# A layer-norm, attention and LoRA layer on eight cores: the adapter selection moved behind the first matmul stage, other buffer counts, and one batched add per tile

## The reference

```python
q = einsum('bse,edh->bsdh', xn, Wq) + bq          # 32 heads of 128
k = einsum('bse,edh->bsdh', xn, Wk) + bk          # 8 heads, each repeated 4 times
v = einsum('bse,edh->bsdh', xn, Wv) + bv          # 8 heads, each repeated 4 times
scores = einsum('bsdh,bseh->bsde', q, k) / sqrt(128)
out = einsum('bsde,bseh->bsdh', softmax(scores), v)
y = einsum('bsd,od->bso', xn, weight) + bias      # 4096 -> 4096
lo = (xn A[adapter]^T) B[adapter]^T               # LoRA, rank 16, one of 3 adapters, by batch
```

## Time and profile before

| what | us |
|---|---|
| median of 3 runs | 1700.04 (1696.85 to 1707.28) |
| the profiled execution | 1697.85 |
| its span on the slowest core (core 4) | 1696.2 |
| spans of the 8 cores | 1690.7 to 1696.2 |
| DVE's first layer-norm reduction | 58.40 |
| stage 2's first matmul | 193.17 |
| stage 2's last matmul, xa's first | 859.59 |
| stage 4's first matmul | 908.28 |
| stage 5's first score matmul | 1381.70 |
| last store issued | 1680.5 |

### The profile page before, as it was taken

One profiled execution on the slowest core, in us unless ns is written; L12 is line 12 of the kernel. 1 busy time (PEld: TensorE's weight loads), 2 busy tenths in 40 slices (PEclk: granted clock), 3 DMA queues, 4 the chain that ended last, 5 costly groups with the idle time before them and its releaser, 6 DMA issues.

```text
span 1696.2 us, 20151 instructions; the slowest of 8 cores (1690.7 to 1696.2 us)
## 1 busy us (share of the span) xinstructions
PE 1380.9 (81%) x8600; PEld 690.2 (41%) x8705; DVE 270.0 (16%) x291; ACT 499.3 (29%) x497; POOL 185.4 (11%) x111
## 2 busy tenths in 40 slices
PE   0022699999999999999977999999999967756553
PEld 0011344444444444444433444444444435644442
DVE  2799200000000000000000000000000015544434
ACT  0255300111011103333343333333333345544442
POOL 1000011111111111111100111111110111011110
PEclk9999999999999999999987999999999975555555
DMA  5633087888888887777774777777777866899998
GB/s 113 84 120 148 1 75 75 75 78 75 78 79 79 79 78 76 75 75 75 75 89 74 71 72 72 72 74 75 75 75 75 84 81 91 105 113 133 120 132 117
DMA packets 503959, 144.77 MB, mean 85 GB/s; under 512 B 498672, under 2 KB 498704, under 8 KB 502800
## 3 DMA queue, kind: packets, MB, share of 16 engines
q0 software_dynamic: 337856, 101.53, 59.5%
q1 hardware_dynamic: 166016, 41.95, 15.1%
HBM read 207.20 MB, written 20.97 MB: 135 GB/s over the span
## 4 chain that ended last, share of the span: by engine, by line
PE 70%; DMA 11%; DVE 8%; issue 5%; ACT 3%; POOL 1%; SPq 0%; ACTq 0%; DVEq 0%; POOLq 0%
PE qk_ps L412 37%; PE f_ps L558 26%; PE s_ps L705 3%; DMA out<-xasm 3%; DVE lnst L272 2%; DVE lnst L267 2%; DVE sqscr L268 2%; ACT ebf L744 2%; DMA wsl<-wall 2%; PE a_ps L722 2%; DMA xasm<-x_in 1%; DMA qkscr<-tsb 1%; DMA a_all<-ah 1%; DMA out<-xasm_e 1%; PE f_ps L563 1%
## 5 line engine op out<-in xcount | busy, mean ns | idle before, releaser
L412 PE MATMUL qk_ps<-xnT,wsl 128*128 128x512 bf16 x3010 | 662.2, 380 | 5.6 <-ACT xnT L316 1.3
L412 PEld LDWEIGHTS qk_ps<-xnT,wsl 128*128 128x128 bf16 x3072 | 300.7, 98 | 366.9 <-issue 7.1
L558 PE MATMUL f_ps<-xnT,wsl 128*128 128x512 bf16 x2005 | 446.1, 380 | 4.6 <-ACT tsb L509 2.2
L558 PEld LDWEIGHTS f_ps<-xnT,wsl 128*128 128x128 bf16 x2048 | 198.1, 98 | 250.3 <-issue 16.9
L588 ACT ACTIVATE ffno<-f_ps,fb_sb 128x512 f16<-128x512 f32 x64 | 152.4, 2629 | 299.1 <-PE f_ps L563 299.1
L757 DVE RECIPROCAL rdb<-b_ps 128x16 f32<-128x16 f32 x64 | 16.2, 253 | 1345.7 <-PE b_ps L725 1273.7
L744 ACT ACTIVATE ebf<-s_ps 128x512 bf16<-128x512 f32 x256 | 139.7, 595 | 148.2 <-PE s_ps L705 147.9
L705 PE MATMUL s_ps<-qst,kst 8*128 8x128 bf16 x1024 | 136.1, 298 | 54.9 <-ACT ebf L744 38.7
L385 POOL DMA_DIRECT2D wsl<-wall x48 | 80.5, 1677 | 703.0 <-PE qk_ps L412 703.0
L442 ACT ACTIVATE qsks<-qk_ps,bqss 128x512 bf16<-128x512 f32 x16 | 36.8, 2537 | 354.0 <-PE qk_ps L412 354.0
L332 PE MATMUL tr_ps<-id_sb,xn 128*128 128x128 bf16 x256 | 33.9, 302 | 121.2 <-ACT xn L308 112.3
(11 more groups left out here) (65 smaller groups left out, 404.5 us busy)
## 6 DMA issues: line engine op xcount, KB each, us to landing
wsl<-wall POOLq DMA_DIRECT2D x80, 1024.0 KB, 12.2
xt<-x_in SPq DMA_DIRECT2D x8, 2048.0 KB, 8.8
xasm<-x_in POOLq DMA_DIRECT2D x10, 1024.0 KB, 14.1
out<-xasm SPq DMA_DIRECT2D x10, 1024.0 KB, 18.2
xasm_e<-x_in POOLq DMA_DIRECT2D x6, 1024.0 KB, 13.7
out<-xasm_e SPq DMA_DIRECT2D x6, 1024.0 KB, 16.4
qkscr<-tsb SPq DMA_DIRECT2D x16, 256.0 KB, 2.6
qst<-qkscr SPq DMA_DIRECT2D x32, 64.0 KB
```

What stands on the lines that cost most here:

```text
L412: mm = t.matmul(qk_ps[bank + half][:], wsl[ft % 2][:, c * P:(c + 1) * P], xnT[:, c * TPC + half * 512: c * TPC + (half + 1) * 512], start= ...
L558: t.matmul(f_ps[bank + half][:], wsl[ft % 2][:, c * P:(c + 1) * P], xnT[:, c * TPC + half * 512: c * TPC + (half + 1) * 512], start=(c == ...
```

## The change

Four things are changed together.

1. The adapter selection leaves the start. DVE begins with two short memsets (epsc, lnst) and the layer norm. The masks, bias sums and the memset of vall stand behind the last layer-norm tile. The broadcast of the masks (ps_h), the copy to hbc and the six mixing steps stand at the end of stage 2, between weight tile 47 and the xa matmuls. POOL loads a_all and the three B matrices, each now with a buffer of its own, behind weight tile 47; so its first two weight loads stand directly behind the seven small loads. TensorE waits for the small loads ahead of its first transpose.
2. Stage 1 has three x buffers instead of two.
3. Stage 5 has two buffers each for qst and kst instead of three; a chunk's load waits for the scores of the chunk two before.
4. In stage 5 the eight results of a tile go to slices of one buffer tmpa_full, and one add of 128x4096 after the eighth replaces the eight adds of 128x512. The wait for the x tile's load stands ahead of that add, and no longer ahead of the first step.

```diff
-        xt = [... for i in range(2)]
+        xt = [... for i in range(3)]
...
+        @block.gpsimd
+        def _(g):
...
+            g.dma_start(out=bsel_sb[:], in_=bsel_d).then_inc(GQ.h, 16)
+            GQ.n += 7 * 16
...
+        @block.vector
+        def _(v):
+            v.memset(epsc[:], EPS).then_inc(VEC.h, 1); VEC.n += 1
+            v.memset(lnst[:], 0.0).then_inc(VEC.h, 1); VEC.n += 1
...
             def _(sy):
                 for tt in range(NT):
-                    if tt >= 2:
-                        sy.wait_ge(SCA.h, p1_norm_mark[tt - 2])
+                    if tt >= 3:
+                        sy.wait_ge(SCA.h, p1_norm_mark[tt - 3])
...
             @block.tensor
             def _(t):
+                t.wait_ge(GQ.h, p0_gq)
                 for tt in range(NT):
...
+        @block.gpsimd
+        def _(g):
+            for ft in range(NQKV):
...
+            g.wait_ge(SCA.h, p1_trev_mark[NT - 1])
+            g.dma_start(out=a_all[:].rearrange("p (c a r) -> p c a r", c=CH, a=3),
+                        in_=ah_d.rearrange("c p a r -> p c a r")).then_inc(GQ.h, 16)
+            GQ.n += 16
+            for a in range(3):
+                g.dma_start(out=bsl[a][:], in_=bh_d[a]).then_inc(BS.h, 16)
+            BS.n += 3 * 16
...
                         mm.then_inc(TEN.h, 1)
                         TEN.n += 1
+                    t.wait_ge(VEC.h, p0b_mask_mark)
+                    t.matmul(ps_h[:], ones_r[:], h3b[:], start=True, stop=True)\
+                        .then_inc(TEN.h, 1)
+                    TEN.n += 1
                     t.wait_ge(VEC.h, p0_vec)
                     for c in range(CH):
...
                         if j == 0:
-                            s.wait_ge(VEC.h, p0_vec)
+                            s.wait_ge(VEC.h, p0b_mask_mark)
...
+                    s.wait_ge(TEN.h, p0_ten)
+                    s.activation(hbc[:], ps_h[:], AF.Copy).then_inc(SCA.h, 1)
                     s.wait_ge(TEN.h, p2_ten_end)
...
+                @block.vector
+                def _(v):
+                    v.wait_ge(SCA.h, p0_sca)
+                    v.wait_ge(GQ.h, p0b_gq)
...
-            qst = [p5sb(f"qst{i}", [NJ, 32 * P]) for i in range(3)]
-            kst = [p5sb(f"kst{i}", [NJ, 32 * P]) for i in range(3)]
+            qst = [p5sb(f"qst{i}", [NJ, 32 * P]) for i in range(2)]
+            kst = [p5sb(f"kst{i}", [NJ, 32 * P]) for i in range(2)]
...
                 for cki in range(4 * NT):
-                    if cki >= 3:
-                        sy.wait_ge(TEN.h, ten_schunk(cki - 3))
+                    if cki >= 2:
+                        sy.wait_ge(TEN.h, ten_schunk(cki - 2))
...
                 for tt in range(NT):
-                    v.wait_ge(XS[tt % 3].h, xs_mark(tt))
                     for sub in range(8):
...
-                        v.wait_ge(VEC.h, VEC.n)
-                        v.tensor_tensor(xasm[tt % 3][:, sub * 512:(sub + 1) * 512],
-                                        xasm[tt % 3][:, sub * 512:(sub + 1) * 512],
-                                        tmpa[0][:], ALU.add).then_inc(VEC.h, 1)
-                        VEC.n += 1
+                    v.wait_ge(XS[tt % 3].h, xs_mark(tt))
+                    v.wait_ge(VEC.h, VEC.n)
+                    v.tensor_tensor(xasm[tt % 3][:], xasm[tt % 3][:],
+                                    tmpa_full[:], ALU.add).then_inc(VEC.h, 1)
+                    VEC.n += 1
```

More of the change, by code:

```diff
@@ L83, in build @@
         vall = sbr("vall", [P, TPC * 9], BF16)
+        ps_h = ctx.enter_context(nc.psum_tensor("ps_h", [P, 3], F32))
         xasm_e = sbr("xasm_e", [P, P * 32], F32)
[L85 to L88, removed]
         xaT_guard = nc.sbuf_tensor("xaT", [16, TPC], BF16)
@@ L345, in build @@
         p1ctx.close()
+        aselt_guard = nc.sbuf_tensor("aselt", [P, CH * 16], BF16)
+        aselt = aselt_guard.__enter__()
+        bselt_guard = nc.sbuf_tensor("bselt", [16, 32 * P], BF16)
+        bselt = bselt_guard.__enter__()
+        p0bctx = ExitStack()
+        a_all = p0bctx.enter_context(nc.sbuf_tensor("a_all", [P, CH * 48], BF16, side="right"))
+        bsl = [p0bctx.enter_context(nc.sbuf_tensor(f"bsl{i}", [16, 32 * P], BF16, side="right"))
+               for i in range(3)]
+        p0b_vec0 = 2 + NT * 9
@@ L466, in build, with _ @@
                 p2_sca_end = SCA.n
-                assert p2_sca_end == p2_sca0 + 50
+                p0_sca = p2_sca0 + 49
+                assert p2_sca_end == p2_sca0 + 51
+                @block.vector
+                def _(v):
+                    v.wait_ge(SCA.h, p0_sca)
+                    v.wait_ge(GQ.h, p0b_gq)
+                    av = a_all[:].rearrange("p (c a r) -> p c a r", c=CH, a=3)
+                    sv = aselt[:].rearrange("p (c r) -> p c r", c=CH)
+                    v.tensor_scalar(sv, av[:, :, 0, :], hbc[:, 0:1], None, ALU.mult)\
+                        .then_inc(VEC.h, 1); VEC.n += 1
+                    for a in (1, 2):
+                        v.wait_ge(VEC.h, VEC.n)
+                        v.scalar_tensor_tensor(sv, av[:, :, a, :], hbc[:, a:a + 1], sv,
+                                               ALU.mult, ALU.add).then_inc(VEC.h, 1); VEC.n += 1
+                    for a in range(3):
+                        v.wait_ge(BS.h, 48)
+                        if a == 0:
+                            v.tensor_scalar(bselt[:], bsl[a][:], hbc[0:16, 0:1], None, ALU.mult)\
+                                .then_inc(VEC.h, 1); VEC.n += 1
+                        else:
+                            v.wait_ge(VEC.h, VEC.n)
+                            v.scalar_tensor_tensor(bselt[:], bsl[a][:], hbc[0:16, a:a + 1],
+                                                   bselt[:], ALU.mult, ALU.add)\
+                                .then_inc(VEC.h, 1); VEC.n += 1
+                        assert p0_b_vec_mark[a] == VEC.n, (a, p0_b_vec_mark[a], VEC.n)
+                assert VEC.n == p0_vec, (VEC.n, p0_vec)
             p3_ten0, p3_sca0 = TEN.n, SCA.n
```

253 lines of the change are left out of this document (108 added, 145 removed).

## The result

The changed kernel takes 1691.0 us (median of 12 runs, 1688.1 at the least) against 1701.98 for the kernel before: ratio 0.9942, interval 0.9928 to 0.9956. By the ratio it is faster by 10 us, and the interval doesn't reach 1; 22 were forecast, and over 1% (17 us) was held likely. Some runs of both kernels, and of three kernels further down, were disturbed and lie far above the rest; the medians take all runs in, the ratios leave these out.

A forecast was written before the change was run, and what follows sets the result against it. TensorE's weight streaming in stages 2 and 4 is 63% of the chain, untouched; time lies at the joints. -46.3 + 19.9 + 4 = -22.4 from 1697.85 gives 1675.5, put at 1677; range 1656 to 1694.

The forecast's parts named there:

- Part 1, the start: Stage 1 start: first layer-norm reduction moves from 58.40 to 12.1 us, 46.3 us gained.
- The lower bound: Start: weight tiles and third x tile hold x tile 0 back until 19.9, so the gain is 38.5 us.
- Part 2, the end of stage 2: Before the xa matmuls: TensorE idles 17.9 us through the selection, then 2.0 for its slow start; cost 19.9.
- Part 3, stage 5: Stage 5: x-load waits go, but chunk loads wait behind stores with two buffers; about 0, taken as +4 us.
- the prediction's own timeline: Stage 5: store 0 at 1453, store 1 at 1484, four periods of 38.8 to 1639, last store landed at 1696.
- D: Stage 5: a store's time from first issue to landing, taken as 25 us; period = D + 13.8 = 38.8.
- A: Rival, stage 5: stores land after 21 us instead of 25, giving 1653; chance 0.14.
- B: Rival: x tile 0 held back at the start, or bsl loads late at stage 2's end; 8 us, 1685; chance 0.15.
- C: Rival, stage 5: stores and x loads share bandwidth, D = 35, period 48.8, giving 1723; chance 0.05.
- The forecast's case: Whole kernel: the forecast itself, 1677 us, against its rivals; chance 0.65.
- D = 29: Stage 5's upper bound: stores taking 29 us would make the stage cost +20 us.
- Faster by over 1%: Whole kernel: time under 1683 us, given 0.67.

The follow-up runs named there:

- the two-buffer run: The changed kernel with two x buffers in stage 1, as before, instead of three: 1691.2 us, ratio 0.9953 to the kernel before.
- the early selection: The changed kernel with masks' broadcast before weight tile 8, a_all and B matrices loaded behind weight tile 20: 1671.1 us, ratio 0.9841 to the kernel before.
- the last kernel: The changed kernel with three q/k buffers, adapter selection done well before weight tile 47 ends, and stage 5 stores in quarters: 1620.2 us, ratio 0.9534 to before.

## Why the prediction failed, point by point

- **Part 1, the start: right.** 47.3 us against 46.3, with x tile 0 landing after 10.0 us. The lower bound (weights and third tile hold tile 0 back) didn't come: tile 0 did not wait for the weights, the weights waited. The third buffer was worth nothing, as said and as the two-buffer run shows. What moved behind the last tile stayed hidden.
- **Part 2, the end of stage 2: right.** 17.5 and 1.9 measured, 17.9 and 2.0 in the sum; the early selection gave 20 back. Between the joints the cost is 17.3, as stages 2 and 3 ran 2.2 shorter, for no known reason. a_all landed 16.6 us after its issue at 785.9, in time.
- **Part 3, stage 5: the mechanism was right, its size was not, and this is the step that failed.** "About 0; I take +4" measured +20.7. Against the prediction's own timeline, counted from the stage's start: store 0 was put at 76.4 us (1453 - 1376.6) and went out at 83.9; store 1 was put 31 later and went out 39.7 later; the four periods of 38.8 (155 in all) were 41.0 (164.0); the tail of 57 was 52.8. That is +7.5, +8.7, +9.0 and -4.2, together 21.0.
  - The first term is one that was left out: chunk loads landed for free until the first store. Beside the x loads they took 10.5 and 12.7 us, and TensorE waited 2.2 and 3.8 for them, so two buffers cover 8 to 9 us. The run without those x loads gives the 7 back.
  - The second, the first period: store and chunk took 21.3 instead of 18.7, TensorE stood 2.5 us within the next scores with no releaser shown, and SP took 2.3 us for one kst.
  - The third, the four later periods: D was put at 25, if anything too high; the stores landed 23.1 to 24.7 us after their first issue. But the chunk's data landed not 1.2 but some 3 us behind the store (kst issued 21.8 us behind store 1 and landed 4.9 later, 26.7 in all, against 23.9 for the store), so that D and the chunk were 27.0 on average instead of 26.2. The scores up to the next load took 13.1 instead of 12.6. And SP's two loads ahead of each store took 0.9 us, which the sum had at nothing. Together 2.2 per period. Each is small; each comes once per tile on a path where nothing is spare.
  - The comparison itself hid the price. I compared the new period with the old one, 39.2, and called it a draw. But the old period was set by the x load wait, and the same change removed that: the measure of what two buffers cost is the kernel with the late x wait and three buffers, whose stores are 35.3 apart and which is 38 us faster.
- **Rivals.** A (stage 5 gains) and B (the start gains less) did not come. C, stores that take 35 us, was the right place with the wrong lever: it needed longer stores to cost anything, while the loss came at D near 24. The forecast's case got 0.65 and the range reached 17 us up; 1691 lies within it, near its upper end, by its width and not by a reason: the +20 for stage 5 had been given to D = 29, and it came at a D of 23 to 25. "Faster by over 1%" at 0.67 was the claim that failed.

The Trainium skill's rule that the DMA engines go round-robin between queue rows (DMA: Bandwidth & Descriptors, Queues, rings and completion order) had been weighed for x tile 0. There no run shows it. It fits where I did not apply it: the q/k loads beside x loads from the other queue, 10.5 to 12.7 us. The larger part is the q/k load's place behind the store in SP's list and queue: of the changed kernel's 70.6 us of waits for kst, 10.3 are the stage's first load, 6.0 fall beside the x loads ahead of the first store, and 54 at the chunks behind stores.

## What to carry to other kernels

When a change removes one wait and thins out another resource, price the second against the kernel in which the first wait is already gone, not against today's period. A small load that is issued in order behind a large store inherits the store's whole time (here 26.7 us from the store's issue to the chunk's landing). Cut the store into pieces and interleave them, or keep enough buffers to cover it: here each was worth some 40 us, and both led to the same 35 us a tile. And where buffers take only a few partitions, several can share one tile's columns at different partitions, so that depth need not be traded for room.

## What the runs showed of the hardware

- SP's issue of a transfer of many pieces is not free: a store of two halves of 8192 pieces held SP for 14.6 us, and the 64 KB load behind it for 7.1. As quarters between the chunks each store held it 0.4 us (2.1 at most), but the load behind up to 7.8, and up to 11.4 in the last kernel: part of the cost moves to the next transfer in the queue.
- POOL issued one transfer of 8192 pieces at a time, each when the one before had landed: issues 11.7 to 15.9 us apart for loads and stores alike. Weight loads of 4096 pieces went out 1.7 us apart.
- Loads of 64 KB in 256-byte pieces landed in 4.9 us behind a store and in 10.5 to 12.7 us beside x loads of 128-byte pieces, while an x tile of 16 KB rows landed in 10.0 us beside the first weight loads, which themselves took 30.8 and 42.0 us.
- After 17.5 us of idleness TensorE ran its first matmuls at 1.2 GHz with the granted clock at 0.50; at the start of stage 2 nine matmuls ran at the same pace with the clock shown as 1.00.
- TensorE's granted clock stayed at 0.50 all through stage 5, even where it was busy for 77% of the time (154.0 of 200 us in the last kernel above). No run here raised it.
